# Block-sparse attention with a low-rank feed-forward layer on one core: the bias row folded into the corner block's product, transpositions in pairs, statistics and a weight piece moved

## The chip, the cores and the metric

The kernel runs on one core of a Trainium2 chip. The metric is the device time in microseconds of one execution, as the median of several runs. The engines are TensorE (PE in the profile, its weight loads PEld), VectorE (DVE), ScalarE (ACT), GpSimd (POOL) and SyncE (SP), on whose queue this kernel issues all its DMA transfers.

## The reference

```python
mod = (_silu(L0_c) @ L0_wmod).reshape(L0_c.shape[0], 6, 1, -1)
sa, ca, ga, sb, cb, gb = (mod[:, 0], mod[:, 1], mod[:, 2], mod[:, 3], mod[:, 4], mod[:, 5])
...
h = _layernorm(x, axis=-1) * (1 + ca) + sa
x = x + ga * _L0_attn_ref(h, ...)      # gelu(h @ ((w1 w2^T) * sparse_mask) + b2)
h = _layernorm(x, axis=-1) * (1 + cb) + sb
x = x + gb * _L0_ffn_ref(h, ...)       # P = h U1; H = P V1 + b1; (silu(gate) * up) U2 V2 + b2
```

`x` is 8 batches of 512 tokens by 1024 features, in float32. The mask keeps a band around the diagonal. The low-rank layer has rank 256 and an inner width of 2752.

## The kernel before, in words

Every float32 operand of a product is split into a high part and a rest (`_hi`, `_lo`), and a product is three matmuls: high x high, high x low, low x high. Tokens come in tiles of 128, four to a batch (`TT`), features in blocks of 128, eight to a batch (`FB`), and outputs in halves of 512 (`h` is 0 or 1).

The program has three stages, one after the other, each a loop over the eight batches.

1. **Attention.** The banded matrix `attn` is made first. Then, for batch b, ScalarE normalizes the tiles of x (`norm`, writes `nrm`), TensorE transposes a block of four tiles (`turn(t, k)`), ScalarE scales the result into `h_hi` (`hi`) and VectorE makes the rest `h_lo` (`lo`). A unit `y(b, u)` is one token tile and one output half: `y_near` multiplies the blocks of the band (`y_part`, three matmuls each), and `y_end` adds the bias row `beta` by one more matmul of 512 columns, with a column of `pick` spread over the tokens as the stationary operand. In each half, one of the five blocks reaches over the half's border by 70 columns only: block 4 in half 0 (the last part of the unit), block 3 in half 1 (its first). I call it the corner. ScalarE then does `gelu`, GpSimd multiplies by the gate and adds x (`gated`), VectorE does some of the additions (`add`), and SyncE stores x2 (`x2_store`) and loads the next x (`next_x`). Between units TensorE transposes the next batch's blocks, and for batches 1 to 6 computes a chunk of the modulation (`mod_product`). In batch 7 ScalarE and VectorE split the matrix U1 as well (`u1_part`), and TensorE makes the second bias (`beta2_product`).
2. **Low-rank stage.** The tiles of x2 come back from DRAM (`next_x2`), t is now 8 + b. Each block is normalized, transposed, split, and multiplied by U1 (`p_product`, six matmuls of 512 columns). The order on TensorE is `turn(t, 4 + k)`, `p_product(b, k)` for k from 0 to 3, then `turn(t + 1, k)`, `p_product(b, 4 + k)`. Three PSUM banks rotate for the transpositions, so each waits for the `lo` of the one three before. The result is split (`pt_hi`, `pt_lo`) and stored (`pt_store`). The statistics for layer norm are VectorE's: of x2 tiles 0 and 1 they are made in the attention stage from the copy on the chip (`stats2`, `aggregate2`), of tiles 2 and 3 in the low-rank stage from the reloaded tiles (`stats`, `aggregate`). GpSimd turns them into `rstd` and `shift`.
3. **Feed-forward stage.** 22 blocks a batch, and the output. The weights V1 and U2 come in pieces through three `raw` buffers (`raw_load`), are split by ScalarE (`weight_hi`) and GpSimd (`weight_lo`); pieces 0 to 4 are converted before this stage and the rest in its first batch.

Nothing schedules this at run time: every engine runs its instructions in the order written, and semaphores hold it back.

## Time and profile before

| | |
|---|---|
| median of 3 runs | 1170.33 us (1170.17 to 1173.3) |
| the profiled execution's own time | 1172.08 us |
| its span, first to last instruction | 1170.3 us |
| mean granted TensorE clock | 0.996 of full |
| TensorE busy | 1142.7 us, 98% |
| VectorE, ScalarE, GpSimd busy | 588.5, 490.1, 390.5 us |

The span is what the profile's rows cover; the time outside it, 1.78 us, is start and end. "Busy" counts an engine's own instructions, not its waits. A matmul's duration in the rows is longer than its distance to the next, since matmuls overlap: what one costs is read from the distance of the starts.

### The profile page before, as it was taken

The page shows a single profiled execution, that of the slowest core. Times are in us where ns is not written, and L with a number is a line of the kernel's source. Part 1 is how long each engine was busy: PE and PEld are TensorE (multiplying, and loading weights), DVE is VectorE, ACT ScalarE, POOL GpSimd, SP SyncE. Part 2 cuts the span into 40 slices and gives each one's busy share as a digit, 9 for nine tenths or more (in the row PEclk, how much of TensorE's full clock was granted, in tenths as well). Part 3 has the DMA queues.
Part 4 walks back from the last instruction along what each step waited for, and adds up shares of the span by engine and source line. Part 5 has one row for each costly group of instructions (what it writes and reads, how often), then busy time and mean ns, then how long its engine had stood idle before and what let it go on. Part 6 is the DMA issues. An engine that isn't in the chain of part 4 may idle for free.

```text
span 1170.3 us, 15391 instructions
## 1 busy us (share of the span) xinstructions
PE 1142.7 (98%) x5883; PEld 946.7 (81%) x5883; DVE 588.5 (50%) x941; ACT 490.1 (42%) x789; POOL 390.5 (33%) x339
## 2 busy tenths in 40 slices
PE   5899999999999999999999999999999999999998
PEld 4668989987888788888888888888888888888886
DVE  3568777885663335444434444343443434344344
ACT  2137767777886544233224224223322432432331
POOL 1028998971113765302113031221302113021210
PEclk9899999999999999999999999999999999999999
DMA  9997888777536541501321040140123105013001
GB/s 359 394 348 261 305 328 323 252 259 251 220 140 219 164 164 73 180 1 72 97 84 73 20 160 1 73 155 26 72 66 115 56 16 180 1 73 109 35 1 72
DMA packets 57484, 169.59 MB, mean 145 GB/s; under 512 B 6208, under 2 KB 11072, under 8 KB 55360
## 3 DMA queue, kind: packets, MB, share of 16 engines
q1 hardware_dynamic: 57408, 168.57, 40.1%
q8 instruction: 49, 0.80, 0.3%
q14 instruction: 27, 0.22, 0.1%
HBM read 126.51 MB, written 42.04 MB: 144 GB/s over the span
## 4 chain that ended last, share of the span: by engine, by line
PE 88%; DMA 3%; SPq 2%; DVE 2%; POOL 2%; issue 1%; ACT 1%; DVEq 0%; POOLq 0%; ACTq 0%
PE bank L546 22%; PE bank L548 21%; PE bank L547 21%; PE bank L728 8%; PE bank L609 4%; PE bank L930 3%; PE bank L937 2%; PE bank L932 2%; PE bank L583 2%; DMA w2t_sb<-in_w2t 1%; PE bank L714 1%; POOL g L1603 1%; SPq L379 1%; POOL xs L1606 1%; PE bank L910 1%
## 5 line engine op out<-in xcount | busy, mean ns | idle before, releaser
L1169 ACT ACTIVATE act<-bank,b_sb 128x512 f32<-128x512 f32 (+1 forms) x176 | 121.3, 690 | 497.3 <-PE bank L548 481.4
L1518 DVE SCALAR_TENSOR_TENSOR act<-bank,b_sb,act 128x512 f32<-128x512 f32 (+1 forms) x176 | 132.0, 750 | 376.3 <-PE bank L548 353.2
L546 PE MATMUL bank<-pt,v_hi 128*128 128x512 f32 x688 | 268.6, 390 | 0.0
L547 PE MATMUL bank<-pt,v_hi 128*128 128x512 f32 x688 | 267.8, 389 | 0.0
L548 PE MATMUL bank<-pt,v_lo 128*128 128x512 f32 x688 | 267.6, 389 | 0.0
L1674 POOL TENSOR_TENSOR x2t<-gbb_bc,x2t 128x512 f32<-128x512 f32 x64 | 86.5, 1374 | 244.8 <-DMA x2t<-x_dram 244.8
L1528 DVE TENSOR_TENSOR act_lo<-act,act_hi 128x512 fp32r<-128x512 f32 (+1 forms) x176 | 160.4, 912 | 0.8
L546 PEld LDWEIGHTS bank<-pt,v_hi 128*128 128x128 f32 x688 | 129.1, 188 | 29.5 <-DVE act L1518 2.6
L548 PEld LDWEIGHTS bank<-pt,v_lo 128*128 128x128 f32 x688 | 129.2, 188 | 26.9
L547 PEld LDWEIGHTS bank<-pt,v_hi 128*128 128x128 f32 x688 | 129.2, 188 | 26.7
L546 PE MATMUL bank<-act_hi,u_hi 128*128 128x512 f32 x336 | 131.0, 390 | 0.7 <-DVE act_lo L1528 0.6
L548 PE MATMUL bank<-act_hi,u_lo 128*128 128x512 f32 x336 | 130.7, 389 | 0.0
L547 PE MATMUL bank<-act_lo,u_hi 128*128 128x512 f32 x336 | 130.7, 389 | 0.0
L1664 POOL TENSOR_TENSOR v_lo<-v2g,v_hi 128x512 fp32r<-128x512 f32 x32 | 43.6, 1364 | 233.2 <-ACT v_hi L1187 233.2
L1375 DVE SCALAR_TENSOR_TENSOR h_lo<-bank,table,h_hi 128x512 fp32r<-128x512 f32 x128 | 93.7, 739 | 54.8 <-ACT h_hi L1023 54.8
L1180 ACT ACTIVATE act_hi<-act 128x512 fp32r<-128x512 f32 (+1 forms) x176 | 109.8, 624 | 7.0 <-DVE act L1518 6.9
L983 ACT ACTIVATE nrm<-xs,shift,rstd 128x512 f32<-128x512 f32 x128 | 100.3, 809 | 15.5 <-POOL shift L1591 15.4
L1023 ACT ACTIVATE h_hi<-bank,table 128x512 fp32r<-128x512 f32 x128 | 86.8, 685 | 47.1 <-PE bank L609 44.4
L1603 POOL TENSOR_TENSOR g<-g,ga_bc 128x512 f32<-128x512 f32 x64 | 84.4, 1321 | 37.3 <-ACT ga_bc L1043 27.6
L728 PE MATMUL bank<-attn_hi,h_hi 128*128 128x198 f32 (+2 forms) x320 | 91.6, 286 | 0.0
L728 PE MATMUL bank<-attn_hi,h_lo 128*128 128x198 f32 (+2 forms) x320 | 89.8, 281 | 0.0
L728 PE MATMUL bank<-attn_lo,h_hi 128*128 128x198 f32 (+2 forms) x320 | 89.7, 281 | 0.0
(134 smaller groups left out, 1663.3 us busy)
## 6 DMA issues: line engine op xcount, KB each, us to landing
xs<-in_x SPq DMA_DIRECT2D x32, 512.0 KB, 5.2
wm_sb<-in_wmod SPq DMA_DIRECT2D x8, 2048.0 KB, 10.8
x_dram<-xs SPq DMA_DIRECT2D x32, 512.0 KB, 5.3
xs<-x_dram SPq DMA_DIRECT2D x32, 512.0 KB, 5.9
x2t<-x_dram SPq DMA_DIRECT2D x32, 512.0 KB, 4.0
out<-x2t SPq DMA_DIRECT2D x31, 512.0 KB, 4.9
pt_dram<-pt_st SPq DMA_DIRECT2D x8, 1024.0 KB, 4.3
pt<-pt_dram SPq DMA_DIRECT2D x8, 1024.0 KB, 5.6
```

Of the source, the lines that this page charges most:

```text
L546: nc.tensor.matmul(acc, s_hi, m_hi, start=start, stop=False)
L547: nc.tensor.matmul(acc, s_hi, m_lo, start=False, stop=False)
L548: return nc.tensor.matmul(acc, s_lo, m_hi, start=False, stop=stop)
L728: nc.tensor.matmul(acc, moving[:, slot, toks], weight[:, s, a:e], start=start and i == 0, stop=False, skip_group_check=True)
L983: nc.scalar.activation(nrm[:, n, cols], source(t)[:, n, cols], ACT.Identity, scale=rstd[:, t, n:n + 1], bias=shift[:, t, n:n + 1]).then_in ...
L1023: nc.scalar.activation(h_hi[:, i % RING, :], bank[:, turn_bank(i), :], ACT.Copy, scale=table[:, t % NB, col:col + 1]).then_inc(hi_ready, 1)
L1169: nc.scalar.activation(act[0:w, j % 2, :], bank[0:w, j % 2, :], ACT.Silu, bias=b1_sb[0:w, i, 0:1]).then_inc(silu_done, 1)
L1180: nc.scalar.activation(act_hi[0:w, slot, :], act[0:w, j % 2, :], ACT.Copy).then_inc(act_hi_ready, 1)
L1375: nc.vector.scalar_tensor_tensor(h_lo[:, i % RING, :], bank[:, turn_bank(i), :], table[:, t % NB, col:col + 1], h_hi[:, i % RING, :], ALU. ...
L1518: nc.vector.scalar_tensor_tensor(act[0:w, j % 2, :], up, b1_sb[0:w, i, 1:2], act[0:w, j % 2, :], ALU.add, ALU.mult).then_inc(act_done, 1)
L1528: nc.vector.tensor_tensor(act_lo[0:w, slot, :], act[0:w, j % 2, :], act_hi[0:w, slot, :], ALU.subtract).then_inc(act_lo_ready, 1)
L1603: nc.gpsimd.tensor_tensor(g[:, n, :], g[:, n, :], ga_bc[:, cols], ALU.mult).then_inc(g_ready, 1)
```

## The change

Four edits.

- **The bias row folded into the corner's product.** For batches 1 to 7 the corner's high x high product is no longer a matmul of 70 columns. The rows of `h_hi` that the corner uses (at most 70 of 128, 96 are taken) are copied into a tile `corner` together with rows of `pick`, and its rows of `attn_hi` into a tile `fold` together with the two rows of `beta`. The one matmul of 512 columns that added the bias now multiplies `corner` by `fold` and adds both. ScalarE makes `corner` for each batch (`corner_pick`, `corner_rows`: five copies of 512 columns), GpSimd, TensorE and ScalarE make `fold` once in the first batch. `beta` moved to other memory.
- **Transpositions two by two** in the low-rank stage: `turn`, `turn`, `p_product`, `p_product`.
- **The statistics of x2** are now all made in the low-rank stage from the reloaded tiles; `stats2` and `aggregate2` are gone. On SyncE's queue the reload for batch 3 goes ahead of the first `raw` loads, and the sixteen small writes of the gates come one batch later, behind the next reload.
- **Weight piece 5** is loaded before the last `pt_store`, not after it, and it and the pieces behind it are converted one block later in the first feed-forward batch.

```diff
@@ y_end @@
-                if b == 0 and n == 0:
-                    pe.wait_ge(pick_made, 3)
-                    pe.wait_ge(beta_lo_ready, h + 1)
-                nc.tensor.matmul(bank[:, n, :], pick[:, b:b + 1].to_broadcast([P, P]),
-                                 beta[:, h * HALF:(h + 1) * HALF], start=False, stop=True,
+                if b == 0:
...
+                    return
...
+                if n == 0:
+                    pe.wait_ge(corner_ready[h], (2 + h) * b)
+                    if b == 1:
+                        pe.wait_ge(fold_made, 4)
+                        pe.wait_ge(fold_ready, h + 1)
+                nc.tensor.matmul(bank[:, n, :], corner[:, h, toks], fold[:, h, :], start=False, stop=True,
                                  skip_group_check=True).then_inc(y_done, 1)
@@ y_part @@
+                terms = [(h_hi, attn_hi), (h_hi, attn_lo), (h_lo, attn_hi)]
+                if b > 0 and part == CORNERS[h][:3]:
+                    del terms[0]
@@ low-rank stage, TensorE @@
-                for k in range(4):
+                for k in (0, 2):
                     turn(t, 4 + k)
+                    turn(t, 5 + k)
                     p_product(b, k)
...
+                    p_product(b, k + 1)
@@ ScalarE @@
+            def corner_pick(b, h):
+                ae.wait_ge(y_done, (b - 1) * 8 + (h + 1) * TT)
...
+                rows = CORNERS[h][3]
+                nc.scalar.activation(corner[rows, h, :], pick[rows, b:b + 1].to_broadcast([SPARE, TOK]),
+                                     ACT.Copy).then_inc(corner_ready[h], 1)
+
+            def corner_rows(b, h):
+                i = b * FB + CORNERS[h][0]
+                ae.wait_ge(hi_ready, i + 1)
+                ae.wait_ge(y_done, (b - 1) * 8 + (h + 1) * TT)
+                for rows in ((slice(0, KEPT),), (slice(SPARE, 2 * SPARE), slice(2 * SPARE, P)))[h]:
+                    nc.scalar.activation(corner[rows, h, :], h_hi[rows, i % RING, :],
+                                         ACT.Copy).then_inc(corner_ready[h], 1)
...
                 norm(b + 1, 0, 0)
                 split(0)
+                corner_pick(b, 1)
                 gelu(b, 1)
+                corner_rows(b, 1)
                 norm(b + 1, 0, 1)
@@ first feed-forward batch, ScalarE @@
-                    if at_start(b, EARLY + i - 1 < PIECES):
-                        weight_hi(EARLY + i - 1)
+                    if at_start(b, 1 < i < PIECES - EARLY + 2):
+                        weight_hi(EARLY + i - 2)
@@ VectorE, low-rank stage @@
                 lo(t, 5)
-                if b == 0:
-                    stats2(NB - 1, 0)
+                if b + 2 < NB:
+                    stats(t + 2, 0)
                 lo(t, 6)
+                if b + 2 < NB:
+                    stats(t + 2, 1)
@@ SyncE, last low-rank batch @@
+                if b == NB - 1:
+                    raw_load(5)
                 pt_store(b)
```

The order on TensorE at the end of a half-0 unit and the start of a half-1 unit, before (a transposition group stands between them):

```order
L728 MATMUL bank<-attn_hi,h_hi 128x70
L728 MATMUL bank<-attn_lo,h_hi 128x70
L728 MATMUL bank<-attn_hi,h_lo 128x70
L714 MATMUL bank<-beta,pick 128x512
L609 MATMUL bank<-ident,nrm 128x128 x4
L728 MATMUL bank<-attn_hi,h_hi 128x70
L728 MATMUL bank<-attn_lo,h_hi 128x70
L728 MATMUL bank<-attn_hi,h_lo 128x70
```

The same place after:

```order
L758 MATMUL bank<-attn_lo,h_hi 128x70
L758 MATMUL bank<-attn_hi,h_lo 128x70
L742 MATMUL bank<-fold,corner 128x512
L615 MATMUL bank<-ident,nrm 128x128 x4
L758 MATMUL bank<-attn_lo,h_hi 128x70
L758 MATMUL bank<-attn_hi,h_lo 128x70
```

One matmul of 70 columns is gone in each unit, and the matmul of 512 columns has other operands.

ScalarE in batch 7, from the first `gelu` of the batch to the last normalization that the first transposition for the low-rank stage needs, before (`g` is gelu, `nrm` the normalization, `u_hi` the split of U1):

```order
L1032 ACTIVATE g<-bank 128x512
L983 ACTIVATE nrm<-xs_81,shift,rstd 128x512
L1049 ACTIVATE u_hi<-u_raw 128x512
L1032 ACTIVATE g<-bank 128x512
L983 ACTIVATE nrm<-xs_81,shift,rstd 128x512 x2
L1032 ACTIVATE g<-bank 128x512
L1049 ACTIVATE u_hi<-u_raw 128x512
L983 ACTIVATE nrm<-xs_81,shift,rstd 128x512
```

The same place after:

```order
L1066 ACTIVATE g<-bank 128x512
L1017 ACTIVATE nrm<-xs_82,shift,rstd 128x512
L1106 ACTIVATE u_hi<-u_raw 128x512
L1092 ACTIVATE corner<-pick 32x512
L1066 ACTIVATE g<-bank 128x512
L1100 ACTIVATE corner<-h_hi 32x512
L1100 ACTIVATE corner<-h_hi 64x512
L1017 ACTIVATE nrm<-xs_82,shift,rstd 128x512 x2
L1066 ACTIVATE g<-bank 128x512
L1106 ACTIVATE u_hi<-u_raw 128x512
L1017 ACTIVATE nrm<-xs_82,shift,rstd 128x512
```

Three copies into `corner` now stand ahead of the last `nrm`.

SyncE from the last stores of x2 to the second `pt_store`, before:

```order
L417 DMA x_dram<-xs_54 128x1024 x2
L433 DMA raw<-in_v 128x2x512 x2
L433 DMA raw<-in_u 128x4x256
L477 DMA gb_dram<-gate_rows 8x128 x8
L480 DMA gbb_dram<-c_pad 8x128 x8
L363 DMA xs_80<-x_dram 128x1024 x4
L427 DMA pt_dram<-pt_st 128x2048
L363 DMA xs_81<-x_dram 128x1024 x4
L427 DMA pt_dram<-pt_st 128x2048
```

And after:

```order
L422 DMA x_dram<-xs_54 128x1024 x2
L368 DMA xs_81<-x_dram 128x1024 x4
L436 DMA raw<-in_v 128x2x512 x2
L436 DMA raw<-in_u 128x4x256
L430 DMA pt_dram<-pt_st 128x2048
L368 DMA xs_82<-x_dram 128x1024 x4
L484 DMA gb_dram<-gate_rows 8x128 x8
L487 DMA gbb_dram<-c_pad 8x128 x8
L430 DMA pt_dram<-pt_st 128x2048
```

The reload of x2 (`xs<-x_dram`) moved ahead of the raw loads, and the sixteen gate writes behind the next reload.

## Rows read from the trace of the kernel before

**Rows 1.** The page, busy time, share of the span and instructions by engine.
```profile
PE 1142.7 (98%) x5883; PEld 946.7 (81%) x5883; DVE 588.5 (50%) x941; ACT 490.1 (42%) x789; POOL 390.5 (33%) x339
```

**Rows 2.** Waits of TensorE, whole span: us in total, times, longest us.
```profile
PE bank L564 <- DMA w2t_sb<-in_w2t: 16.1, 2, 12.3
PE bank L609 <- DVE h_lo L1375: 5.0, 4, 1.9
```

**Rows 3.** The same view, 94 to 104 us.
```profile
PE bank L609 <- DVE h_lo L1375: 2.5, 2, 1.5
```

**Rows 4.** Stages: length, busy PE, PEld, DVE, ACT, POOL, clock, DMA share, GB/s.
```profile
141.59:163.48 21.89, 21.89 (x183) 19.75 (x181) 16.95 (x35) 15.22 (x24) 19.72 (x19) 1.00 0.91 331
...
251.57:375.00 123.43, 120.25 (x638) 99.29 (x639) 73.51 (x129) 92.42 (x139) 23.07 (x35) 0.99 0.58 213
```

**Rows 5.** Timeline, TensorE and its weight loads, 130.5 to 131.8 us.
```profile
130.56 0.19 PEld L728 LDWEIGHTS bank<-attn_hi,h_hi 128*128 128x128 f32 x1
130.65 0.21 PE L728 MATMUL bank<-attn_hi,h_hi 128*128 128x70 f32 x1
130.67 0.19 PEld L728 LDWEIGHTS bank<-attn_lo,h_hi 128*128 128x128 f32 x1
130.70 0.28 PE L728 MATMUL bank<-attn_lo,h_hi 128*128 128x70 f32 x1
...
131.60 0.28 PE L728 MATMUL bank<-attn_hi,h_hi 128*128 128x70 f32 x1
...
131.71 0.28 PE L728 MATMUL bank<-attn_lo,h_hi 128*128 128x70 f32 x1
```

**Rows 6.** The chain that ended last, 139 to 143 us: start, us, what.
```profile
139.15 0.44 PE bank L609 x4
...
141.59 0.87 PE bank L609 x8
```

**Rows 7.** Timeline, low-rank stage, 277 to 288.1 us: TensorE, SyncE and VectorE.
```profile
272.70 1.77 SPq L363 DMA_DIRECT2D xs<-x_dram  x4
...
277.00 0.60 PE L609 MATMUL bank<-ident,nrm 128*128 128x128 f32 x4
...
278.84 0.60 PE L609 MATMUL bank<-ident,nrm 128*128 128x128 f32 x4
...
280.78 1.29 DVE L1236 BATCH_NORM_STATS2 bn<-xs 128x6 f32<-128x512 f32 x2 [5.34 <-DMA xs<-x_dram]
...
282.78 0.66 PE L609 MATMUL bank<-ident,nrm 128*128 128x128 f32 x4 [1.95 <-DVE h_lo L1375]
...
288.07 0.60 PE L609 MATMUL bank<-ident,nrm 128*128 128x128 f32 x4
```

**Rows 8.** The same view as rows 4, 284 to 286 us.
```profile
284.00:286.00 2.00, 2.00 (x8) 1.57 (x7) 1.96 (x6) 0.16 (x1) 0.95 (x3) 0.50 1.02 406
```

**Rows 9.** Timeline, first feed-forward batch: SyncE, ScalarE, TensorE.
```profile
375.10 0.43 SPq L433 DMA_DIRECT2D raw<-in_u  x1
...
381.30 1.06 ACT L1070 ACTIVATE u_hi<-raw 128x1024 fp32r<-128x1024 f32 x1 [3.00 <-DMA raw<-in_u]
...
385.45 0.50 PE L546 MATMUL bank<-act_hi,u_hi 128*128 128x512 f32 x1 [0.64 <-DVE act_lo L1528]
```

**Rows 10.** Timeline, attention: ScalarE in batch 4, then ScalarE and TensorE in batch 7.
```profile
153.33 0.60 ACT L1032 ACTIVATE g<-bank 128x512 f32<-128x512 f32 x1 [2.74 <-PE bank L714]
...
237.49 0.63 ACT L1049 ACTIVATE u_hi<-u_raw 128x512 fp32r<-128x512 f32 x1
238.01 0.81 ACT L983 ACTIVATE nrm<-xs,shift,rstd 128x512 f32<-128x512 f32 x1
...
238.88 0.66 PE L609 MATMUL bank<-ident,nrm 128*128 128x128 f32 x4
```

**Rows 11.** Timeline, low-rank stage: TensorE's turn(t, 4) and VectorE's lo(t, 5).
```profile
300.90 0.60 PE L609 MATMUL bank<-ident,nrm 128*128 128x128 f32 x4
...
305.09 0.74 DVE L1375 SCALAR_TENSOR_TENSOR h_lo<-bank,table,h_hi 128x512 fp32r<-128x512 f32 x1
```

More of the change, by code:

```diff
@@ L296, in p_bank @@
             return (7, 3)[r] if b == NB - 1 else b % 2 * 2 + r
-        def pieces_of(t):
-            return range(TT) if t < NB else range(TT // 2, TT)
         UP = INTER + width[-1]
@@ L491, in _ @@
                     raw_load(4)
+                if b == NB - 1:
+                    raw_load(5)
                 pt_store(b)
-            for m in range(5, PIECES):
+            for m in range(6, PIECES):
                 raw_load(m)
@@ L689, in first_gates, with fold_turn @@
                 last.then_inc(ga_spread, 1)
+            def fold_turn(h):
+                pe.wait_ge(beta_lo_ready, h + 1)
+                pe.wait_ge(ga_first, h + 1)
+                rows = BETA_LO + NB
+                nc.tensor.matmul(bank[0:2 * NB, 6 + h, :], both[0:rows, :], beta[0:rows, h * HALF:(h + 1) * HALF],
+                                 start=True, stop=True).then_inc(fold_turned, 1)
             def y_near(b, u, first=0, last=None):
@@ L726, in y_part @@
                 acc = bank[:, n, a - h * HALF:e - h * HALF]
-                for i, (moving, weight) in enumerate(((h_hi, attn_hi), (h_hi, attn_lo), (h_lo, attn_hi))):
+                terms = [(h_hi, attn_hi), (h_hi, attn_lo), (h_lo, attn_hi)]
+                if b > 0 and part == CORNERS[h][:3]:
+                    del terms[0]
+                for i, (moving, weight) in enumerate(terms):
                     nc.tensor.matmul(acc, moving[:, slot, toks], weight[:, s, a:e], start=start and i == 0,
@@ L795, in first_batch @@
                 turn(1, 1)
+                fold_turn(0)
                 y(0, 7, whole)
+                fold_turn(1)
                 turn(1, 2)
@@ L845, in _ @@
                         beta2_turn()
-                for k in range(4):
+                    p_product(b, k + 1)
+                for k in (0, 2):
                     if b < NB - 1:
                         turn(t + 1, k)
+                        turn(t + 1, k + 1)
                     p_product(b, 4 + k)
+                    p_product(b, 5 + k)
             def h_waits(b, q, j):
@@ L979, in norm @@
                     ae.wait_ge(turned, (t - 1) * FB + c * 4 + 4)
-                if c == 0 and n not in pieces_of(t):
-                    ae.wait_ge(*source_in(t, n))
                 cols = slice(c * HALF, (c + 1) * HALF)
@@ L1097, in _ @@
             gelu(0, 6)
+            fold_rows(0)
             hi(1, 2)
             hi(1, 3)
+            fold_rows(1)
+            corner_pick(1, 0)
             gelu(0, 7)
@@ L1103, in _ @@
                 hi(b, 4)
-                for k in range(5, FB):
-                    hi(b, k)
+                hi(b, 5)
+                corner_rows(b, 0)
+                hi(b, 6)
+                hi(b, 7)
                 if b == 5:
@@ L1120, in _ @@
                 split(2)
+                if b < NB - 1:
+                    corner_pick(b + 1, 0)
                 for k in range(4):
```

146 lines of the change are left out of this document (86 added, 60 removed).

## The prediction

> **What bounds the kernel now.** I read the page's busy times first, then the waits of TensorE, then busy times by stage, then the timeline inside single steps. TensorE is busy 98% of the span [rows 1], so almost every microsecond of the end time is a TensorE microsecond. Where it does wait, it waits for the first weights to arrive (16.1 us, untouched here) and for `h_lo` on VectorE (5.0 us in four places) [rows 2]. By stage [rows 4], one attention batch takes 21.89 us with TensorE busy for all of it, GpSimd for 19.72 and ScalarE for 15.22; in the low-rank stage (251.57 to 375) TensorE loses 3.2 us. So there are two ways to gain: TensorE work taken out, and the few stalls. There are two ways to lose: work put on ScalarE and VectorE that makes TensorE wait, and a clock that falls after a wait.
>
> **The corner's matmul.** For the batches 1 to 7, eight units each, the 70-column product `h_hi`x`attn_hi` goes: 56 matmuls. The bias matmul stays one 128x512 matmul, with other operands. What is one small matmul worth? In [rows 5] the weight loads around it start 0.11 us apart (130.56, 130.67) for a stream of only 70 columns. At the head of an h=1 unit the matmuls start 0.11 apart as well (131.60, 131.71). At the end of an h=0 unit the first of the two starts 0.05 before the next (130.65, 130.70), but its weight load still takes its 0.11 place. I take the load's pitch: 56 x 0.11 = 6.2 us less. The lower bound uses 0.05 for the 28 of h=0: 28 x 0.05 + 28 x 0.11 = 4.5. The 6.2 is 0.88 a batch; 21.0 remain.
> The Trainium skill ("TensorE: Matmul & The Clock Gate", section "Wait — 56ns, not 53.3ns?") gives a warm matmul N ÷ 2.4 GHz plus 2.5 ns, an estimated 32 ns for 70 columns and 1.8 us for 56 of them. By that rule the sum below would end near 1167.3. The trace of before does not agree: it shows 0.11 a piece.
>
> **New small work at the start.** TensorE gets two `fold_turn` matmuls in the first batch, at most 0.3 us each; right behind them it waits for `h_lo` anyway (2.5 of the 5.0 us lie there [rows 3]), so nothing is added; without that cover it would be 0.6. GpSimd's preparations end long before its first gated product. I take 0, with 0 to +0.6.
>
> **ScalarE in the attention batches.** Five copies a batch are new (`corner_pick` two, `corner_rows` one and two). A copy of that width holds ScalarE 0.52 us: `u_hi` starts at 237.49, the next instruction at 238.01 [rows 10]. Together 2.6 us; 15.22 + 2.6 = 17.8 of 21.0, so they fit on the average. Three of them stand ahead of the last normalization for the next batch's first transposition, `turn(b+1, 0)`. In batches 1 to 6 TensorE runs the modulation product between, and ScalarE sits idle for 2.74 us behind its last normalization (153.33 [rows 10]). Batch 7 has no such product, and ScalarE also has `u1_part`. There, before the change, the last normalization runs 238.01 to 238.82 and the transposition starts at 238.88 [rows 10]: no slack is left. After the change it ends 3 x 0.52 = 1.56 later, at 240.4, while TensorE comes four matmuls earlier, at 238.88 - 0.44 = 238.44. New stall: 1.9 us, once. Queued behind it on TensorE is all of the second half of batch 7. Bounds: 0 to +1.9.
> Later in that batch VectorE makes `u1_lo` from later `u_hi` parts, and `beta2_product` waits for it, and the statistics of x2 now come from reloaded tiles. I take +0.4 for these, 0 to +1.
>
> **The clock.** In the low-rank stage a wait of 2.1 us was followed by a granted clock of 0.50 (1.2 GHz) [rows 8]. Its cost: the two transposition periods from 282.78 to 288.07 take 5.29 us, where an undisturbed one (277.00 to 278.84) takes 1.84; 5.29 - 3.67 = 1.6 us [rows 7]. The new stall of 1.9 us is near that length. Between 0 and 1.6, I take +0.8.
>
> **The statistics and the order on SyncE's queue.** In the low-rank stage one transposition should have started at 278.84 + 1.84 = 280.68 and started at 282.78 [rows 7]: 2.1 us late, and 1.6 more by the clock, 3.7 in all. The chain behind it: SyncE issued `raw` loads and sixteen small gate writes first, and the tiles of x2 for batch 3 only at 272.70; VectorE's statistics waited for them until 280.78; `h_lo` stands behind the statistics in its queue. After the change that load is issued right when its buffer is free, several us earlier, and the gate writes come a batch later, behind the next load. So this stall goes: -3.7 (0 to -3.7).
> The price is on VectorE: the statistics of tiles 0 and 1 moved out of attention into this stage (count unchanged: four fewer there per batch, four more here, 0.64 us each by the pair at 280.78 [rows 7]). Does TensorE then wait? Let S be the start of `turn(t, 4)`. Before, `lo(t, 5)` starts at S + 4.2 (300.90, 305.09) [rows 11], behind ScalarE's work, whose order is unchanged. After: `lo(t, 5)` 0.74, two statistics 1.28, `lo(t, 6)` 0.74, ready at S + 7.0; then 1.28 + 0.74 + 1.28 + 0.74, `lo(t+1, 0)` ready at S + 11.0. TensorE: a pair of transpositions 0.87, a product 1.84 - 0.44 = 1.40; the second transposition of the third pair, which needs `lo(t, 6)`, is at S + 7.8, that of the fourth, which needs `lo(t+1, 0)`, at S + 11.4. Slacks 0.8 and 0.4 us. Cost 0, but tight.
>
> **Two by two.** A single transposition group costs 0.44 us on the chain, a pair 0.87 [rows 6]. Nothing is gained by pairing. What it does is to bring the second of each pair 1.4 us forward, as used above. 0.
>
> **The weight piece.** In the first feed-forward batch ScalarE waited 3.00 us until 381.30 for piece 5, the SiLU behind it came late, and TensorE waited 0.64 us until 385.45 [rows 9]. The load was issued at 375.10, behind `pt_store`. After: issued ahead of it, as soon as piece 2 is converted, and converted itself one block later. Piece 5 is needed four blocks on. -0.6 (0 to -0.6). Behind it the pieces keep a distance of three blocks to their use.
>
> **Sum.** -6.2 - 3.7 - 0.6 + 1.9 + 0.4 + 0.8 = -7.4 us. The profiled execution took 1172.08 us with a span of 1170.3, so it would take 1164.7; the median of the three runs stands 1.75 lower, at 1170.33, and gives 1162.9: **1163**.
>
> **Rivals.**
> - *No new stall in batch 7* (ScalarE's copies on few partitions are cheaper, or idle time takes them): the terms +1.9, +0.4, +0.8 fall, 1159.8. For it: ScalarE is only 15.22 of 21.89 busy; against it: the zero slack of [rows 10].
> - *The old low-rank stall stays or moves*: the x2 tiles still land late, since VectorE's last `add` of batch 7 is now one statistics pair later and its store must land before the reload; or the first two tiles, now needed 1.28 us earlier in VectorE's order, aren't there. -3.7 becomes about -0.3: 1166.3.
> - *The corner's matmul was nearly free*: only its 0.05 us of [rows 5] counts, 56 x 0.05 = 2.8 in place of 6.2: 1166.3. [...]
> - *GpSimd or ScalarE holds the attention period at 21.89*: GpSimd has 19.72 busy and a period of 21.0 leaves it 1.3. Then 6.2 is lost: 1169, no change that can be told.
> - *Slower: VectorE becomes the bound of the low-rank stage.* The slacks of 0.4 and 0.8 us are used up by longer statistics, and in each of six batches two transpositions wait. It decides against the change once each such wait exceeds (7.4 + 3.5) / 12 = 0.9 us; at 1 us each, +12: 1175.
>
> **How the numbers follow.** Forecast 0.40, no new stall 0.22, old stall stays 0.13, matmul nearly free 0.05, attention held 0.10, VectorE bound 0.10. What a measurement of this kernel can tell from no change is about 0.3%, 3.5 us. Faster than 1166.8: 0.40 + 0.22, and 0.10, 0.04 and 0.01 of the next three, 0.77. Slower than 1173.8: 0.08 of the last. Same: 0.15. The range takes in the first four cases (0.80): from the second with its rounding, 1158.5, to the third and fourth with the bound of 4.5 for the matmuls, 1168. The likeliest case's own range is 1161 to 1165.
>
> **What would show it.** Attention batches 2 to 6 should repeat every 21.0 us; 56 fewer 70-column matmuls, and loads still 0.11 apart. The first transposition for the low-rank stage (in batch 7) should show TensorE waiting about 1.9 us for ScalarE's `nrm`, and the granted clock near it may show 0.50. The low-rank stage should have no wait over 0.5 us and no fall of the clock, and a period of 14.7 us a batch. In the feed-forward stage the 0.64 us wait should be gone. The prediction is wrong if the attention period is above 21.4, or if the second transpositions of pairs wait for `h_lo`.

## The result and the profile after

The changed kernel takes 1175.52 us (median of 12 runs, 1174.22 to 1177.63), against 1170.4 for the kernel before (12 runs on the same chip, 1169.12 to 1173.3): ratio 1.0038, 95% interval 1.0026 to 1.0049. It is slower by 0.4%, where the prediction had 1163 us and a range of 1158.5 to 1168. Its profiled execution has a span of 1174.3 us against 1170.3.

TensorE's waits in the changed kernel, to be read beside [rows 2] (us in total, times, longest):

```profile
PE bank L570 <- DMA w2t_sb<-in_w2t: 16.6, 2, 12.2
PE bank L552 <- issue: 5.3, 1, 5.3
PE bank L615 <- DVE h_lo L1430: 3.2, 3, 1.6
PE bank L615 <- issue: 2.4, 1, 2.4
PE bank L615 <- ACT nrm L1017: 2.1, 1, 2.1
```

The second and the fourth row have no partner of that size in the kernel before, which has one wait of 1.2 us under "issue", that is, a wait for nothing that the profile shows. No step of the prediction spoke of either. Both lie where the attention ends and the low-rank stage begins. The timeline of TensorE there, before and after:

```profile
251.16 0.41 PE L714 MATMUL bank<-beta,pick 128*128 128x512 f32 x1
252.80 0.63 PE L609 MATMUL bank<-ident,nrm 128*128 128x128 f32 x4 [1.23 <-issue]
253.18 0.48 PE L546 MATMUL bank<-h_hi,u_hi 128*128 128x512 f32 x1
```

```profile
252.09 0.42 PE L742 MATMUL bank<-fold,corner 128*128 128x512 f32 x1
254.88 1.17 PE L615 MATMUL bank<-ident,nrm 128*128 128x128 f32 x8 [2.37 <-issue]
261.33 0.80 PE L552 MATMUL bank<-h_hi,u_hi 128*128 128x512 f32 x1 [5.29 <-issue]
261.93 0.63 PE L553 MATMUL bank<-h_lo,u_hi 128*128 128x512 f32 x1
```

From the last unit of `y` to the first low-rank product it is 2.02 us before (251.16 to 253.18) and 9.24 after (252.09 to 261.33). And it isn't over there: the products' matmuls start 0.42 to 0.60 apart, where they start 0.23 apart in the kernel before, since the clock is at 1.2 GHz (granted 0.50) after the wait. Windows of the changed kernel, columns as in [rows 4]:

```profile
256.00:261.00 5.00, 0.04 (x1) 0.00 (x0) 2.69 (x4) 2.92 (x5) 0.00 (x0) 0.50 0.95 306
261.00:266.00 5.00, 4.67 (x12) 3.32 (x13) 0.00 (x0) 0.00 (x0) 0.00 (x0) 0.50 0.19 76
```

From the first window: for five microseconds TensorE does nothing while the DMA engines are 95% busy. The low-rank stage and the feed-forward stage as windows that begin with the first product of each, before and after:

```profile
253.18:372.36 119.18, 117.23 (x626) 96.67 (x624) 71.65 (x125) 89.40 (x134) 21.36 (x32) 0.99 0.58 216
372.36:1170.30 797.94, 793.73 (x3505) 651.40 (x3503) 339.51 (x443) 259.42 (x428) 207.65 (x145) 1.00 0.24 80
```

```profile
261.33:377.34 116.01, 116.01 (x619) 97.69 (x620) 79.61 (x150) 84.52 (x129) 18.87 (x28) 0.98 0.56 207
377.34:1174.30 796.96, 793.44 (x3505) 651.43 (x3503) 337.56 (x443) 259.56 (x428) 208.17 (x145) 1.00 0.23 80
```

So the span's +4.0 us is made up of: the attention from batch 1 on +1.1 (before 97.45 to 251.16, after 97.30 to 252.09), the passage between the stages +7.2, the low-rank stage -3.2, the feed-forward stage -1.0, and -0.15 ahead of batch 1. The passage alone turns a gain into a loss.

The attention is the second surprise. These are its repeats, by the start of `turn(b, 4)`, in batches 2 and 3:

```profile
118.49 1.04 PE L615 MATMUL bank<-ident,nrm 128*128 128x128 f32 x8
...
139.74 1.04 PE L615 MATMUL bank<-ident,nrm 128*128 128x128 f32 x8
```

Batches 2 to 6 take 21.25, 21.01, 21.20, 21.04 and 22.49 us in place of 21.89, and batch 7 takes 26.6 us up to its last unit in place of 22.2. What batches 1 to 5 gain, the last two give back, and 1.1 more.

### The profile page after: what moved, and what is told of

Read it like the earlier page. It is cut to its first block, busy times and chain, and to the rows that moved or that the text cites. A ratio compares the mean times of both kernels' runs of the same rounds, so it can differ in the third digit from the quotient of the medians.

```text
span 1174.3 us, 15327 instructions
## 1 busy us (share of the span) xinstructions
PE 1139.3 (97%) x5829; PEld 943.1 (80%) x5829; DVE 580.5 (49%) x938; ACT 509.9 (43%) x826; POOL 394.4 (34%) x347
## 4 chain that ended last, share of the span: by engine, by line
PE 78%; issue 0%; ACT 0%; DVE 0%; DVEq 0%; ACTq 0%
PE bank L552 22%; PE bank L554 22%; PE bank L553 22%; PE bank L966 3%; PE bank L973 2%; PE bank L968 2%; PE bank L615 2%; PE bank L758 1%; PE bank L946 1%; ACT nrm L1017 0%; DVE act L1569 0%; DVE act_lo L1579 0%; PE bank L742 0%; PE bank L620 0%; PE bank L621 0%
## 5 line engine op out<-in xcount | busy, mean ns | idle before, releaser
L1017 ACT ACTIVATE nrm<-xs,shift,rstd 128x512 f32<-128x512 f32 x128 | 100.3, 808 | 22.5 <-POOL shift L1640 22.3
L758 PE MATMUL bank<-attn_hi,h_lo 128*128 128x198 f32 (+2 forms) x320 | 88.0, 283 | 0.0
L758 PE MATMUL bank<-attn_lo,h_hi 128*128 128x198 f32 (+2 forms) x320 | 87.8, 278 | 0.0
L1301 DVE BATCH_NORM_STATS2 bn<-xs 128x6 f32<-128x512 f32 x128 | 81.3, 679 | 6.0 <-DMA xs<-in_x 6.0
```

Source lines behind the costliest of these rows:

```text
L758: nc.tensor.matmul(acc, moving[:, slot, toks], weight[:, s, a:e], start=start and i == 0, stop=False, skip_group_check=True)
L1017: nc.scalar.activation(nrm[:, n, cols], source(t)[:, n, cols], ACT.Identity, scale=rstd[:, t, n:n + 1], bias=shift[:, t, n:n + 1]).then_in ...
```

## The experiments

**Theory A**: the two waits are TensorE waiting for its own instructions. The branch for masks with entries outside the band (`If(dense != 0)`, over 3,000 matmuls) is never taken with these inputs, so at the end of the attention TensorE jumps over it. I call the place where its program goes on the landing; the first thing there is the transpositions of the low-rank stage. **A1** says that instructions come in blocks, and that the long wait comes because the changed kernel's shorter code puts the landing just ahead of a block's edge; **A2** that the block comes late because its load shares the DMA engines with the reload of x2. **Rival B**: something invisible, such as a semaphore behind SyncE's transfers, holds TensorE. For the attention: **theory G**, the fold's gain is all there and lost again in VectorE's and ScalarE's queues; the rival is that a corner matmul was nearly free.

**e1, without the jump.** Nothing that is executed changes.

```diff
-            with nc.tensor.If(dense != 0):
-                first_batch(True)
-                for b in range(1, NB):
-                    attention(b, True)
```

> The changed kernel without the second branch of TensorE's program, the one for masks with entries outside the band: the code is left out, so that TensorE, when the seven attention batches are done, does not jump over some 3,000 instructions but goes straight on to the low-rank stage. With these inputs that branch is never taken, so nothing that is executed changes. Theory A (the two waits for nothing visible after the attention, 2.4 us at 254.9 and 5.3 us at 261.3, are TensorE waiting for its instructions after the jump): both are gone or under 0.5 us, the stretch of half clock behind them too, and the kernel takes 1175.5 - 7.7 - 2 = about 1166 us. Rival B (something that the profile does not show as a releaser holds TensorE there, for example a semaphore from SyncE's transfers): the waits stay, and it takes 1175 us.

1166.14 us (1164.21 to 1167.27), ratio to before 0.9958 (0.9948 to 0.9969). Both waits are gone; so are 9.4 us. Rival B falls: the data and the semaphores are the same.

**e2, e16, e17: filler in code that is never run.**

```diff
                 for b in range(1, NB):
                     attention(b, True)
+                for i in range(64):      # 12 in e16, 4 in e17
+                    nc.tensor.transpose(bank[:, i % 4, 0:P], nrm[:, 0, 0:P], ident[:])
```

> The changed kernel with 64 more transpositions written at the end of the branch that is not taken; nothing that is executed changes, only the place in the program at which TensorE lands after the jump. Theory A1 (instructions come in blocks, and the second wait of 5.3 us comes because the landing place lies a few instructions ahead of the end of its block): the waits change in place or length by more than 1 us, either one near 2.4 us alone (about 1168 us in all) or a second one elsewhere. Theory A2 (the wait is set only by what the transfers of that moment do to the instruction load): same waits within 1 us, 1175 us. Rival B (not instructions): same waits, 1175 us.

> The changed kernel with only 12 more transpositions at the end of the branch that is never taken. The second wait came 8 matmuls behind the landing; when the landing itself lies 12 further on, the edge of the block is behind TensorE. Theory A1: the second wait is gone and one wait of 1.2 to 2.4 us is left, 1169.6 us, the same as with 64. If 12 change nothing: 1175.5 us, and the place does not count in such small steps.

> The changed kernel with 4 more transpositions at the end of the branch that is never taken. Theory A1: the landing is 4 matmuls nearer to the edge of its block, so the second wait comes behind 4 transpositions and not behind 8, with the first product no longer the one that waits, and is 5 to 6 us long: about 1175.5 us. If the place where TensorE stops is set by data or by a semaphore of the first product: behind 8 as before.

With 64: 1169.63 us, ratio 0.9986 (0.9975 to 0.9997). With 12: 1169.31 us, ratio 0.9986 (0.9976 to 0.9995). With 4: 1176.54 us (one run). The timelines after the landing, of e16 and of e17:

```profile
255.41 1.06 PE L615 MATMUL bank<-ident,nrm 128*128 128x128 f32 x8 [1.30 <-issue]
256.23 0.48 PE L552 MATMUL bank<-h_hi,u_hi 128*128 128x512 f32 x1
```

```profile
255.62 0.63 PE L615 MATMUL bank<-ident,nrm 128*128 128x128 f32 x4 [1.56 <-issue]
261.89 1.01 PE L615 MATMUL bank<-ident,nrm 128*128 128x128 f32 x4 [5.64 <-issue]
262.55 0.77 PE L552 MATMUL bank<-h_hi,u_hi 128*128 128x512 f32 x1
```

Four transpositions of filler move the long wait from behind the eighth transposition to behind the fourth. Twelve put the landing past the edge, and the long wait is gone. The wait hangs on a place in the code, matmul by matmul.

**e4, one block and one product in turn.**

```diff
-                for k in (0, 2):
-                    turn(t, 4 + k)
-                    turn(t, 5 + k)
-                    p_product(b, k)
-                    p_product(b, k + 1)
+                for k in range(4):
+                    turn(t, 4 + k)
+                    p_product(b, k)
```

> The changed kernel with the low-rank stage's order put back to one transposed block and one product in turn. It is the pairing alone that is undone. If pairing is worth nothing by itself and does not move the waits: 1175 us. If the second wait of 5.3 us hangs on how many instructions stand between the landing place and the first product (four transpositions in place of eight), it moves or shrinks: the clock falls less, and the kernel takes 1168 to 1171 us. My reading of the trace, 0.15 us gained by pairing in each of eight batches, would add 1.2 us here.

1176.64 us, ratio 1.0044 (1.0027 to 1.0062). After the landing:

```profile
255.52 0.63 PE L615 MATMUL bank<-ident,nrm 128*128 128x128 f32 x4 [1.71 <-issue]
255.91 0.47 PE L552 MATMUL bank<-h_hi,u_hi 128*128 128x512 f32 x1
256.22 0.39 PE L553 MATMUL bank<-h_lo,u_hi 128*128 128x512 f32 x1
256.45 0.40 PE L554 MATMUL bank<-h_hi,u_lo 128*128 128x512 f32 x1
256.68 0.40 PE L552 MATMUL bank<-h_hi,u_hi 128*128 128x512 f32 x1
263.19 0.80 PE L553 MATMUL bank<-h_lo,u_hi 128*128 128x512 f32 x1 [6.11 <-issue]
```

Four transpositions and four matmuls of products: again eight matmuls behind the landing, though other work now stands there. The middle of a product, whose three matmuls have no semaphore wait between them in the program, cannot be waiting for data. By the medians the pairing is worth 1.1 us, which the intervals don't tell apart from nothing. The undisturbed middle of the stage does: eight blocks take 14.61 us one by one (e4, 301.04 to 315.65) and 14.52 two by two (e16, 303.07 to 317.59), 0.1 us a batch and 0.7 in all eight batches.

**e6, the kernel before brought to the same place.**

```diff
                     for part in far[h]:
+                        if left_out < 51:
+                            left_out += 3
+                            continue
                         y_part(b, u, part, False)
```

> The kernel before, with 51 matmuls left out of the branch that is never taken, so that TensorE, after its jump, lands at nearly the same place of the program, counted in instructions, as the changed kernel does (5474 against 5473 instructions ahead of it). Nothing that is executed changes. Theory A1 (place in the code): the kernel before now shows a second wait of 5 to 6 us, 8 to 20 matmuls behind the landing, half clock behind it, and takes 1170.4 + 6.5 + 1 = about 1178 us. If it is some other property of the changed kernel that makes the wait: 1170.4 us.

1173.59 us, ratio 1.0024 (1.0011 to 1.0036).

```profile
252.58 0.63 PE L609 MATMUL bank<-ident,nrm 128*128 128x128 f32 x4 [1.57 <-issue]
...
258.55 0.22 PE L665 MATMUL bank<-ident,pt_st 8*128 8x8 f32 x1 [3.80 <-issue]
```

The kernel before now has the second wait too, eleven matmuls behind its landing. It is 3.8 us and the loss is 2.8 us against the same chip's 1170.8, not the 7.5 that I expected. Part of the difference is that the old low-rank stall of [rows 7] is gone here: TensorE's waits for `h_lo` come to 2.7 us in all, where the kernel before has 5.0. The wait itself is shorter mostly because TensorE has more to do before it: from the landing to the end of its eleventh matmul it works for 2.2 us, where the changed kernel has 1.2 us of transpositions. The changed kernel's work is not needed for the wait.

**e7, the branches in the other order.**

```diff
-            with nc.tensor.If(dense == 0): ...
             with nc.tensor.If(dense != 0): ...
+            with nc.tensor.If(dense == 0): ...
```

> The changed kernel with its two branches written in the other order: the one for masks with entries outside the band first, the one that is taken with these inputs behind it. The jump over some 3,000 instructions then lies ahead of the first batch, and TensorE goes from the attention straight on to the low-rank stage. Theory A: the two waits at 254.9 and 261.3 are gone (-7.7 us, and -2 for the clock), and one of 1 to 3 us, or of up to 8 if its landing is unlucky, stands ahead of the first batch, where TensorE waits 0.3 us for VectorE's mask anyway: 1167 us, range 1166 to 1173. Rival B: 1175 us.

1172.34 us, ratio 1.0012 (1.0001 to 1.0023). The passage between the stages is clean, but the jump ahead of the first batch now costs 4.6 us under "issue", and the kernel takes 6.2 us more than e1. The jump was moved, and its price with it.

**e8, a quiet DMA at the jump.** A further version, e3, was to put the reload behind the first low-rank product, so that it would stay whole and only come later. In that order the engines wait for each other for ever and it has no time, so e8 cuts the reload's size instead, and leaves out most of that block's data.

```diff
+                if t == NB + 2:
+                    for n in range(TT):
+                        sp.dma_start(source(t)[:, n, 0:16], x2_tiles[t - NB, n][:, 0:16])...
+                    return
```

> The changed kernel with the reload of the third low-rank block's tokens (four transfers of 512 KB, issued from 252.1 us, just as TensorE jumps) cut to four of 8 KB; this leaves out that block's data, and no time of a compute instruction. Theory A2 (the instruction load is slow because it stands in line with that reload): the waits of 2.4 and 5.3 us shrink to 1.2 and under 2 us, and the kernel takes about 1170 us. Theory A1 alone (only the place in the code counts, each wait a fixed latency): the waits stay within 0.5 us, 1175 us.

1173.25 us, ratio 1.002 (1.0009 to 1.0032). The first wait stays at 2.3 us, the second falls from 5.3 to 2.0. The trace shows the blocks themselves: a packet of 0.02 MB on queue q8, "instruction". In the changed kernel one starts in 252.0 to 252.5 and the next in 258.5 to 259.0:

```profile
q8 instruction: 1, 0.02, 11.0%
...
q8 instruction: 1, 0.02, 17.5%
```

TensorE goes on 2.3 to 2.9 us behind each of them, at 254.88 and at 261.33. In e8 the second packet lies in 255.5 to 256.0, three microseconds earlier, and TensorE's product starts at 258.46:

```profile
q8 instruction: 1, 0.02, 16.6%
```

```profile
256.75 0.75 DVE L1434 SCALAR_TENSOR_TENSOR h_lo<-bank,table,h_hi 128x512 fp32r<-128x512 f32 x1 [3.28 <-ACT h_hi L1061]
258.46 0.79 PE L556 MATMUL bank<-h_hi,u_hi 128*128 128x512 f32 x1 [2.03 <-DVE h_lo L1434]
```

The profile puts this wait down to `h_lo`, but the last `h_lo` ends at 257.50, 0.96 us before the product starts, and in batch 6 (below) a transposition starts 0.06 us behind the `h_lo` that it waits for. The packet fits, as in the other cases: TensorE goes on 2.5 to 3.0 us behind its start. So A1 and A2 are both true: the place decides whether TensorE meets the edge, and the traffic of SyncE's reload how long it stands there.

The Trainium skill ("Runtime: NRT & Kernel Launch", section "Instruction fetch mechanics") says that instructions are refilled in order in blocks of 16 KiB by a DMA queue of the engine's own, and that a taken branch outside of the blocks held forces a fetch and a stall. The traces agree on the size and on the stall: the changed kernel's page of the profile has 48 packets with 0.79 MB, 16.5 KB each (next fence), and the stall behind this jump is 1.2 us at its best and 1.7 + 6.1 at its worst.

```profile
q8 instruction: 48, 0.79, 0.3%
```

**e5, the kernel before without the jump**, by the edit of e1.

> The kernel before, without the branch for masks with entries outside the band: nothing that is executed changes, only the jump is gone. Theory A (instruction supply): its one wait for nothing visible, 1.2 us at 252.8, goes, and it takes 1169 us; against the changed kernel without that branch (1166.1) this then gives what the change is worth apart from instruction supply, about -3 us. Rival B: 1170.4 us.

1169.86 us, ratio 0.9992 (0.9979 to 1.0006). Without the jump on either side the change is worth 1166.14 - 1169.86 = -3.7 us, half of the -7.4 forecast.

**e12 and e15, without the fold**; e12 without the jump, e15 with it.

```diff
-                if b > 0 and part == CORNERS[h][:3]:
-                    del terms[0]
...
-                corner_rows(b, 0)
...
-                corner_pick(b, 1)
...
-                corner_rows(b, 1)
...
```

and the bias product of batch 0 for all batches.

> The changed kernel without the second branch (1166.1 us, no jump), and without the fold: eight more 70-column matmuls in each of batches 1 to 7 and the bias row's product in place of the corner block's, no corner copies on ScalarE. The term for the fold stands or falls here: by my forecast 56 matmuls x 0.11 us = 6.2 us more, less the waits that the shorter batch and the copies brought (2.1 for the normalization, 1.7 for h_lo, and up to 2 of half clock): about 1167 to 1169 us. If a corner matmul is nearly free (0.03 us): 1166.1 + 1.8 - 5 = 1163 us.

> The changed kernel with both branches, without the fold: eight more 70-column matmuls in each of batches 1 to 7, the bias row's product in place of the corner block's, no corner copies on ScalarE. TensorE's landing lies 56 matmuls further on in the code than in the changed kernel, so by theory A1 the second wait of 5.3 us is gone: one wait of 1.2 us, no waits for nrm, 1166.2 + 1.5 = about 1167.5 us, that is 8 us faster than the changed kernel, though TensorE multiplies 6.2 us more. If the long wait belongs to something else: 1173 to 1175 us.

e12 takes 1166.15 us, ratio 0.9962 (0.9948 to 0.9976); with the fold it was 1166.14. **The fold is worth nothing that can be told**, where the two intervals together leave about 2 us of doubt, though batches 2 to 5, which run undisturbed, are shorter by 0.64 to 0.88 us each. e15 takes 1167.61 us, ratio 0.9968 (0.9955 to 0.998): with 56 matmuls more than the changed kernel it is 7.9 us faster. Most of that is the long wait, which is gone. The fair partners are e2 and e16, which keep the fold and have a short wait at the landing too: e15 is 1.7 to 2.0 us faster than these, with intervals that overlap at the edge only. Its waits have one "issue" of 1.5, and, as in e12, none for `nrm`.

Where the fold's gain went, the changed kernel's timelines show. VectorE at the end of batch 5, and TensorE there:

```profile
198.10 1.23 DVE L1373 TENSOR_SCALAR gate_big<-gate_size 128x32 f32<-128x32 f32 x1
199.36 1.23 DVE L1374 SCALAR_TENSOR_TENSOR gate_feat<-gate_sign,gate_big 128x32 f32<-128x32 f32 x1
200.51 0.74 DVE L1430 SCALAR_TENSOR_TENSOR h_lo<-bank,table,h_hi 128x512 fp32r<-128x512 f32 x1
201.17 1.27 DVE L1314 TENSOR_TENSOR xs<-g,xs 128x512 f32<-128x512 f32 x1
202.37 1.27 DVE L1301 BATCH_NORM_STATS2 bn<-xs 128x6 f32<-128x512 f32 x2
203.56 0.73 DVE L1430 SCALAR_TENSOR_TENSOR h_lo<-bank,table,h_hi 128x512 fp32r<-128x512 f32 x1
```

```profile
204.35 0.66 PE L615 MATMUL bank<-ident,nrm 128*128 128x128 f32 x4 [0.76 <-DVE h_lo L1430]
```

No row of VectorE has an idle time: it works without a pause, 3.2 us of it on placing a gate chunk (197.27 to 200.51, of which two rows are shown), and the `h_lo` that the next transposition's bank waits for ends at 204.29. With 21.89 us a batch this fitted; with 21.0 it does not. The cost is more than the waits of 0.76 and 0.86 us: from the first to the fourth group of transpositions in a batch TensorE takes 4.41 us in batch 6 (202.99 to 207.40) and 4.51 in batch 7 (225.48 to 229.99), against 2.86 in batch 5 (181.95 to 184.81), so 1.55 and 1.65 us go there. And ScalarE and TensorE in batch 7, the place of the forecast stall:

```profile
235.40 1.52 ACT L1017 ACTIVATE nrm<-xs,shift,rstd 128x512 f32<-128x512 f32 x2
236.83 0.57 ACT L1066 ACTIVATE g<-bank 128x512 f32<-128x512 f32 x1
237.31 0.62 ACT L1106 ACTIVATE u_hi<-u_raw 128x512 fp32r<-128x512 f32 x1
237.82 0.80 ACT L1017 ACTIVATE nrm<-xs,shift,rstd 128x512 f32<-128x512 f32 x1
```

```profile
238.68 1.12 PE L615 MATMUL bank<-ident,nrm 128*128 128x128 f32 x4 [2.07 <-ACT nrm L1017]
```

**e9, e10, e11: the two queues in another order**, on e2, that is, with the 64 fillers, so that the long wait is gone. e9 puts ScalarE's splits behind the last normalization, e10 VectorE's `h_lo` ahead of statistics, e11 does both.

```diff
-                split(0)                          # e9
...
-                split(1)
                 norm(b + 1, 0, 3)
+                split(0)
                 gelu(b, 3)
+                split(1)
                 split(2)
...
-                stats(t, 2)                       # e10, b in (5, 6)
                 lo(b + 1, 2)
+                stats(t, 2)
```

> The changed kernel with the 64 transpositions of padding (its wait for instructions 1.2 us, 1169.6 us), and in batch 7 ScalarE's first two splits of the low-rank weight (0.6 us each) moved behind the last of the four normalizations for the next transpositions, which frees that one by 1.2 us; TensorE waits 2.07 us for it now. Theory C (ScalarE's queue, lengthened by the corner copies, makes that wait, and the half clock behind it is its consequence): the wait falls to 0.9 us, the half-clock stretch behind it goes or shortens, and it takes 1169.6 - 1.2 - (0 to 2) = about 1167.5 us. Rival D (the normalization waits for its inputs, the statistics): same wait, 1169.6 us.

> The changed kernel with the padding, and in batches 5 and 6 VectorE's low half of block b+1, 2 put ahead of one tile's statistics (1.27 us). Theory E (with TensorE's batch shorter, VectorE, which places the gates in these two batches, is late with h_lo, and TensorE waits 0.86 and 0.9 us at the first transposition of the next batch): both waits fall to nothing, 1169.6 - 1.7 = 1167.9 us. Rival F: the statistics that come later hold the next normalization, a wait of 0.5 us or more comes elsewhere, 1169.6 us.

> Both of these orders together, on the changed kernel with the padding: 1169.6 - 2.0 - 1.7 = about 1166 us; this is the version that should beat both kernels, computes all that they compute, and whose two kinds of waits that the change brought are gone. If one of the two only moves the other, 1167.5 us.

e9: 1166.92 us, ratio 0.9973 (0.9963 to 0.9983); the wait for `nrm` falls from 2.1 to 1.0, but `beta2_product` now waits 2.0 us, under "issue". No jump stands ahead of it. VectorE's `u_lo`, which it needs, ends at 246.66, 0.11 us before it starts; the late splits made that late:

```profile
243.63 3.03 DVE L1415 TENSOR_TENSOR u_lo<-u_raw,u_hi 128x512 fp32r<-128x512 f32 x2
246.77 0.28 PE L620 MATMUL bank<-u_hi,sh_hi 128*8 128x256 f32 x1 [1.99 <-issue]
```

So "issue" alone doesn't show that TensorE waits for instructions; what shows it above is where the wait goes when only the code moves.

e10: 1169.31, 0.9985 (0.9976 to 0.9995): the waits move to the next `h_lo`, 1.2 and 1.1 us at L758; nothing is won. e11: 1167.24, 0.9973 (0.9964 to 0.9983), no better than e9.

**e14 and e13: the gate placing where VectorE is idle.** e14, on e2:

```diff
+                if b in (6, 7):        # VectorE, behind lo(b, 7)
+                    mod_place(q - 1)
...
-                if q < NCHUNK:
+                if q < NCHUNK and b < 5:
                     mod_place(q)
```

and the gates' transposition behind `y(7, 3)`. e13 adds the edit of e9, and puts `beta2_product` behind `y(7, 7)` and `beta2_turn` behind `p_product(0, 1)`.

> The changed kernel with the padding (1169.6 us), and of these moves only the placing of the last two gate chunks and the gates' transposition. Theory G: TensorE's waits for h_lo at the start of batches 6 and 7 (0.86 and 0.9 us) go, the period of those batches falls from 22.5 to 21.2 us: 1167.5 us; or, if the wait for nrm in batch 7 grows by what TensorE arrives earlier there, 1168.5 to 1169.6. If h_lo is late for another reason than VectorE's placing: no change, 1169.6 us.

> The changed kernel with the padding (1169.6 us), with ScalarE's splits of batch 7 late as before, and three more moves: VectorE's placing of the last two gate chunks (3.3 us each in the trace, between statistics and h_lo) put behind h_lo of block 7 of the next batch, where VectorE is idle for 4.3 us; the gates' transposition two units of y later; the second bias row's product behind the last unit of y, and its transposition behind the second low-rank product. Theory G (the fold's gain was all there and was given back in VectorE's and ScalarE's queues): the waits for h_lo (0.86, 0.9, 0.3), most of that for nrm (2.07) and the 2.0 us that the late splits brought elsewhere go, with the half clock: 1169.6 - 2.1 - 1.0 - 1.7 = about 1164.5 us. If the work only moves the wait on: 1167 us.

e14: 1167.62 us, ratio 0.9963 (0.995 to 0.9975). The waits at the heads of batches 6 and 7 are gone. But the one for `nrm` grew from 2.1 to 2.7:

```profile
PE bank L615 <- ACT nrm L1019: 2.7, 1, 2.7
```

e13: 1167.35 us, 0.9957 (0.994 to 0.9973), with runs from 1162.98 to 1169.32; batch 6 takes 21.1 us in place of 22.5, and 1.7 us of wait for `nrm` are left. There ScalarE's first normalization waits 0.7 us for GpSimd's `shift`, and the corner's three copies still stand ahead of the fourth.

**e18, batch 7's last corner copies on VectorE**, on e13; the gates' transposition comes one unit of `y` later.

```diff
+                nc.vector.tensor_copy(corner[rows, h, :], pick[rows, b:b + 1].to_broadcast([SPARE, TOK]))...
+                for rows in (slice(SPARE, 2 * SPARE), slice(2 * SPARE, P)):
+                    nc.vector.tensor_copy(corner[rows, h, :], h_hi[rows, i % RING, :])...
```

> The version with all the late moves (1167.35 us), with the last corner copies of batch 7 (0.6 us for the picks and 1.3 for the block's rows) made by VectorE, which was idle 1.8 us soon after, and the gates' transposition one unit of y later. Theory G: the fourth normalization comes 1.9 us earlier, TensorE's wait for it (1.7 us) and the half clock behind it (about 1.5 us) go: 1164 us, and the fold is then worth about 3 us against the same kernel without it (1167.6). If VectorE's own queue is then late (gates, then the transposition or the splits): 1166 to 1168 us.

1168.46 us, ratio 0.9982 (0.997 to 0.9993): by the medians worse than e13, though the intervals overlap. The wait for `nrm` is gone, and VectorE is late instead, two of its copies being far dearer than ScalarE's:

```profile
231.03 2.98 DVE L1356 CAST corner<-h_hi 32x512 fp32r<-32x512 f32 x2
```

`u_lo` ends at 247.37 and `beta2_product` starts at 247.47, after a wait of 1.6 us under "issue" that e13 doesn't have; 0.3 and 0.5 us of wait for `gate_feat` and `h_lo` come before it. The longest wait of e18 is another matter, though the profile names VectorE:

```profile
252.03 0.73 DVE L1443 SCALAR_TENSOR_TENSOR h_lo<-bank,table,h_hi 128x512 fp32r<-128x512 f32 x1
253.57 1.52 PE L615 MATMUL bank<-ident,nrm 128*128 128x128 f32 x8 [3.14 <-DVE h_lo L1443]
```

These are the transpositions at the landing. `h_lo` ends at 252.76, 0.81 us before them, and a packet of instructions starts between 250.75 and 251.0, 2.6 to 2.8 us before them. It is the jump's wait again, which e13 has at the same place with 3.0 us under "issue".

## Why the prediction was wrong

- **The step that failed first is one that the prediction does not have**: its sum costs what instructions do, and puts the passage from the attention to the low-rank stage at nothing without giving a reason, though the edit moves the landing of the jump there. The passage cost 7.2 us more, and 2.0 of half clock behind it (the low-rank stage from its first product is 116.0 us in the changed kernel and 114.0 in e16). e1 gives 9.4 us back by the medians. Shown by e1, e2, e16, e17, e4 and e6; that the reload lengthens it, by e8. The 1.23 us under "issue" at 252.80 were in the trace of before, and could have been the warning. Of the 12.5 us between forecast and measurement this is 9.4; the other 3.1 separate e1 from the forecast, and come from the next points.
- **The corner's matmul, -6.2**: its price of 0.88 us a batch is right in batches 3 and 5 (21.01 and 21.04 us for 21.0 forecast), and it is 0.64 and 0.69 in batches 2 and 4. As a gain for the kernel it is nothing that can be told (e1 against e12). The mistake is in *ScalarE in the attention batches*: I examined ScalarE's slack in batch 7, and put VectorE's in the attention at nothing. VectorE's work at the end of batches 5 and 6 makes TensorE wait 0.76 and 0.86 us for `h_lo` at the head of the next batch, and costs 1.55 and 1.65 us there. e14 shows the placing of the gates as the cause of the two waits.
- **ScalarE in batch 7, +1.9**: measured 2.07, at the place and for the reason forecast. That it depends on ScalarE's order is shown by e9, that the copies bring it by e12 and e15, which have neither the copies nor the wait. The closeness of the size is in part luck: the three copies hold ScalarE 1.83 us and not 1.56 (0.52 from 232.97 to 233.49, and 1.31 from 234.09 to 235.40), and where TensorE isn't held by VectorE before, the wait is 2.7 (e14).
- **The clock after it, +0.8**: from 238.7 to 242.1 the granted clock is 0.51, so 3.4 us are spent on what takes 1.7 at full clock. The cost is 1.7, just above my upper bound of 1.6, which came from the old stall [rows 7]; halving it to 0.8 had no ground in a row.
- **`u1_lo` and the statistics in batch 7, +0.4**: nothing. From 242.60 to 250.03 TensorE takes 7.43 us in the changed kernel, and 7.61 before (241.36 to 248.97).
- **The old low-rank stall, -3.7**: gone, as forecast. The low-rank stage is shorter by 5.2 us in e16 (114.0 against 119.2), 1.5 more than forecast; a period of 14.52 us a batch where the kernel before has 14.67 (300.90 to 315.57) makes 1.2 of them. That the late load was the cause was not tried by itself.
- **Two by two, 0**: -0.7 by the periods of e4 and e16; I had taken no gain from pairing [rows 6]. VectorE did not become the bound: behind 290 us no wait of TensorE is left in the low-rank stage.
- **The weight piece, -0.6**: the wait is gone, and the feed-forward stage measures -1.0.
- **The rivals**: none named the jump. The slower case (1175) came true in its number, by luck: its mechanism, VectorE as the bound of the low-rank stage, isn't there. *The corner's matmul nearly free* is answered by batches 2 to 5, which are shorter by 0.08 to 0.11 us for each of the eight matmuls.

What stays open: why the first wait after the landing lies between 1.2 and 2.4 us with the same code ahead of it (1.2 in e2 and 2.35 in e10, which have the same TensorE program). The packets narrow it down: the first one starts between 252.50 and 252.75 in e16, 1.0 to 1.2 us ahead of the last unit of `y` at 253.70, and in the changed kernel between 252.25 and 252.50, 0.2 to 0.4 behind that unit; TensorE goes on 2.4 to 2.9 us behind the packet in both. What differs is when the fetch begins, not how long it takes. Open is also how much of the fold's 6.2 us a full repair of the last two batches would bring. e13 shows 1167.35 with the fold and e15 1167.61 without, the same within their intervals.

By the medians e2 and e16 stay 3.2 us or more above e1; their profiled executions have spans of 1166.8 and 1167.1 us against 1165.4, which the wait at the landing explains. What scatters between executions of this program shows in the traces: the same wait of 1.6 us at 97 us is followed by a granted clock of 1.00 in the changed kernel's and e2's executions, and of 0.66 over 97 to 102 us in those of e1 and e16, where batch 1 then takes 22.74 us in place of 21.2.

Of the versions that keep both branches, e9, e11, e13, e14 and e15 are the fastest, 0.3 to 0.4% under the kernel before, so each beats both kernels.

## What to carry to other kernels

When an engine's program has a jump over much code, look at the timeline behind the landing before and after every edit: an edit that changes only the number of instructions can move the landing to a block's edge, and here twelve fillers in code that is never run took the long wait away (four did not); keep large transfers away from that moment. When the bound engine is made faster by 4% a period, check every engine's queue in the period in which it has the most work, not its mean busy time. A wait's releaser in a profile is an inference: look whether the named work ended just before the wait did. Here a wait of 2.07 us cost 3.8, since the clock fell behind it.

## What the hardware showed that was not expected

- A block of instructions is a packet of 16.5 KB on queue q8. TensorE went on 2.1 to 3.0 us behind its start, for the first and the second packet alike, in the changed kernel, e4, e6, e8, e16 and e17. With the DMA engines 95% busy the second packet started 6.5 us behind the first, and with the reload cut to 8 KB pieces 3 us.
- The three matmuls of one product were torn apart by 6.1 us in the middle, with every operand ready (e4).
- A wait of 1.6 us at 97 us was followed by half clock in some executions and not in others; with it batch 1 took 1.5 us longer.
- Two copies of 32 and 64 partitions took VectorE 2.98 us (e18, while GpSimd ran its products), where ScalarE takes 1.28 us for the same two (in the changed kernel at 234.09), and VectorE 0.73 us for a whole `h_lo` of 128x512. VectorE's third copy, of a broadcast column of `pick` into 32x512, took 0.40 us, at 230.59, when GpSimd had only small work. What makes the two dear was not tried.
